# Start addresses of matmul operands in a fused attention and feed-forward kernel

## The reference

```python
x = x + tanh(g_xattn[0]) * L0_xattn(layernorm(x), ctx, ctx, W, b)
x = x + tanh(g_ffn[0])   * L0_ffn(layernorm(x), Wg, Wu, Wd)       # 8 experts, 256 -> 1024 -> 256
x = x + tanh(g_xattn[1]) * L1_xattn(layernorm(x), ctx, mask, ...)  # 8 heads of 64
x = x + tanh(g_ffn[1])   * L1_ffn(layernorm(x), wg, W, b)          # routed, 8 experts

def L0_ffn(x, Wg, Wu, Wd):       # the part with the split products
    acc = 0
    for wg, wu, wd in zip(Wg, Wu, Wd):
        acc += (silu(x @ wg) * (x @ wu)) @ wd
```

## The kernel before

| operand | arena | start |
|---|---|---|
| `xop_hi`, `xop_lo` (moving, gate and up) | `sb` | 1376 behind a multiple of 2048 |
| `w_hi`, `w_lo`, `wd_hi`, `wd_lo` (weights of gate, up, down), one block of 128 | `sb` | 352 behind a multiple of 512 |
| `hid_hi`, `hid_lo` (moving, down) | `st` | 256 behind a multiple of 2048 |
| `t_hi`, `t_lo` of T1, T2, T4 (moving, down), T3 lies in `hid` | `sx` | 128 behind a multiple of 2048 |
| `wds_hi`, `wds_lo` (weights, summed, down), one block of 128 | `sx` | 128 behind a multiple of 512 |

## Time and profile before

### The profile page before, as it was taken

The page is one execution under the profiler, slowest core; times in us unless marked ns, Lnnn a source line. Parts: engine busy times, 40 slices in busy tenths (PEclk is TensorE's granted clock), DMA queues, the critical chain, the costliest instruction groups (busy, mean ns, idle before and its releaser), DMA issues.

```text
span 1258.8 us, 18431 instructions
## 1 busy us (share of the span) xinstructions
PE 1232.6 (98%) x6152; PEld 995.4 (79%) x6152; DVE 1054.3 (84%) x1775; ACT 729.2 (58%) x1509; POOL 880.5 (70%) x833
## 2 busy tenths in 40 slices
PE   7999999999999999999999999999999999999998
PEld 5778888888888888888888888888888887787775
DVE  5887889898899999999999999888999974667546
ACT  2455566656666666666666666666566545545543
POOL 3735688888887888888877888888888626443435
PEclk9999999999999999999999999999999999999999
DMA  4020200000110000000000000000100330000131
GB/s 137 26 92 1 94 26 26 26 26 26 41 36 26 26 26 26 26 26 26 26 26 26 26 26 26 26 26 31 42 29 1 117 118 1 18 26 10 35 98 63
DMA packets 42366, 48.28 MB, mean 38 GB/s; under 512 B 4239, under 2 KB 40143, under 8 KB 42015
## 3 DMA queue, kind: packets, MB, share of 16 engines
q1 hardware_dynamic: 38720, 43.07, 10.4%
q0 software_dynamic: 1440, 3.41, 0.8%
q10 hardware_dynamic: 2111, 0.63, 0.2%
HBM read 37.36 MB, written 10.29 MB: 38 GB/s over the span
## 4 chain that ended last, share of the span: by engine, by line
PE 91%; DVE 4%; ACT 3%; issue 1%; DMA 0%; POOLq 0%; ACTq 0%; POOL 0%; DVEq 0%
PE bank L1307 25%; PE bank L1308 25%; PE bank L1309 25%; ACT PC L1050 2%; PE bank L1545 2%; PE bank L1554 1%; PE bank L1269 1%; PE bank L1707 1%; PE bank L1724 1%; PE bank L1251 1%; DVE nmC L2101 1%; PE bank L1529 1%; PE bank L1213 1%; PE bank L1657 1%; PE bank L1479 1%
## 5 line engine op out<-in xcount | busy, mean ns | idle before, releaser
L1307 PE MATMUL bank<-xop_hi,w_hi 128*128 128x512 f32 x896 | 351.9, 393 | 1.7 <-ACT half_g L948 1.2
L1308 PE MATMUL bank<-xop_lo,w_hi 128*128 128x512 f32 x896 | 352.4, 393 | 0.0
L1309 PE MATMUL bank<-xop_hi,w_lo 128*128 128x512 f32 x896 | 351.4, 392 | 0.0
L1958 DVE TENSOR_TENSOR hid_lo<-hid,hid_hi 128x512 fp32r<-128x512 f32 x228 | 220.2, 979 | 14.1 <-ACT hid_hi L972 9.8
L1307 PEld LDWEIGHTS bank<-xop_hi,w_hi 128*128 128x128 f32 x896 | 168.9, 188 | 42.4 <-ACT half_g L948 1.5
L1308 PEld LDWEIGHTS bank<-xop_lo,w_hi 128*128 128x128 f32 x896 | 168.6, 188 | 38.2
L1309 PEld LDWEIGHTS bank<-xop_hi,w_lo 128*128 128x128 f32 x896 | 168.6, 188 | 37.7
L972 ACT CAST hid_hi<-hid 128x512 fp32r<-128x512 f32 x228 | 140.8, 622 | 57.9 <-DVE hid L1950 57.9
L956 ACT ACTIVATE s<-bank 128x512 f32<-128x512 f32 x128 | 78.3, 612 | 102.5 <-PE bank L1309 102.5
L1307 PE MATMUL bank<-hid_hi,wd_hi 128*128 128x512 f32 x344 | 136.2, 396 | 0.6 <-DVE hid_lo L1958 0.6
L1308 PE MATMUL bank<-hid_lo,wd_hi 128*128 128x512 f32 x344 | 136.2, 396 | 0.0
(11 more groups left out here) (273 smaller groups left out, 2615.1 us busy)
## 6 DMA issues: line engine op xcount, KB each, us to landing
raw_gu<-in_L_ffn_Wg_dram SPq DMA_DIRECT2D x32, 256.0 KB, 2.7
raw_gu<-in_L_ffn_Wu_dram SPq DMA_DIRECT2D x32, 256.0 KB, 3.1
raw_d<-in_L_ffn_Wd_dram SPq DMA_DIRECT2D x32, 256.0 KB, 3.7
slots<-empty_row SPq DMA_DIRECT2D x1, 2080.0 KB, 11.1
xr<-slots SPq DMA_DIRECT2D x8, 260.0 KB, 4.5
x_res<-in_x_dram SPq DMA_DIRECT2D x4, 512.0 KB, 5.3
x_mid<-x_res SPq DMA_DIRECT2D x1, 2048.0 KB, 9.2
x_res<-x_mid SPq DMA_DIRECT2D x4, 512.0 KB, 5.4
```

The lines of the kernel that those rows point to most:

```text
L1307: mm(ps, w, a, start=start, stop=False, skip_group_check=True)
L1308: mm(ps, w, a_low, start=False, stop=False, skip_group_check=True)
L1309: return mm(ps, w_low, a, start=False, stop=True, skip_group_check=True)
L1958: nc.vector.tensor_tensor(out=hid_lo[n % 2][h][:], in0=hid[h][:], in1=hid_hi[n % 2][h][:].bitcast(F32), op=ALU.subtract).then_inc(lo_ready ...
```

## The change

No instruction is added, taken out or moved, on any engine: in both programs 11441 instructions stand in the same order with the same shapes, waits and signals. Tiles lie at other addresses. Constants name a row of 2048 bytes and two remainders; `Arena.align` moves an arena's next address up to a remainder.

```diff
+ROW_BYTES = 2048
+OPERANDS_AT = 0
+STATIONARY_AT = 256
...
+    def align(self, residue):
+
+        self.at += (residue - self.at) % ROW_BYTES
+        assert self.at <= self.end, (self.at, self.end)
...
-        x_res = keep.take("x_res", [P, NT, D], F32)
...
+        desc = keep.take("desc", [P, CT, E], F32)
+        keep.align(OPERANDS_AT)
+        x_at = keep.at
+        x_res = keep.take("x_res", [P, NT, D], F32)
         a0_at = keep.at
...
+        sums_at = sa.at + (OPERANDS_AT - sa.at) % ROW_BYTES
...
-        st = Arena(nc, keep.at, sa.at)
+        st = Arena(nc, keep.at, sums_at)
...
         hid_hi, hid_lo = [], []
+        st.align(OPERANDS_AT)
...
-        sx = Arena(nc, base, base + 4 * NT * D)
+        sx = Arena(nc, x_at, x_at + 4 * NT * D)
...
-        m_acc = {i: sm.take(f"m_acc{i}", [P, CH], F32) for i in ("M1", "M5", "M6")}
-
-        sb = Arena(nc, sa.at, end)
+        m_acc = {i: sm.take(f"m_acc{i}", [P, CH], F32) for i in ("M1", "M5", "M6", "M7")}
+
+        sb = Arena(nc, sums_at, end)
         acc = sb.take("acc", [P, KB, T], F32)
+        assert sb.at % ROW_BYTES == OPERANDS_AT
...
         for i in range(2):
+            if i == 0:
+                sb.align(STATIONARY_AT)
             w_at.append(sb.at)
```

More of the change, by code:

```diff
@@ L175, in flamingo_kernel @@
         keep = Arena(nc, base, end)
-        x_res = keep.take("x_res", [P, NT, D], F32)
+        LANES = NC + 3
+        LN_FRONT, LN_FRONT2, LN_ROUTE = range(NC, LANES)
         ident = keep.take("ident", [P, P], F32)
@@ L184, in flamingo_kernel, with norm_lanes @@
         V0 = keep.take("V0", [KH, 2 * B, D], F32)
+        stats, mv, ve, rstd = [], [], [], []
+        def norm_lanes(of):
+            for i in of:
+                stats.append(keep.take(f"stats{i}", [P, CT, 6], F32))
+                mv.append(keep.take(f"mv{i}", [P, CT, 2], F32))
+                ve.append(keep.take(f"ve{i}", [P, CT], F32))
+                rstd.append(keep.take(f"rstd{i}", [P, CT], F32))
+        norm_lanes(range(NC))
         v0_end = keep.at
@@ L191, in flamingo_kernel @@
         betac = keep.take("betac", [P, KB], F32)
[L193 to L198, removed]
+        norm_lanes(range(NC, LANES))
         wgr = keep.take("wgr", [P, KB, E], F32)
@@ L204, in flamingo_kernel @@
         tg_ffn = keep.take("tg_ffn", [P, 2], F32)
-        desc = keep.take("desc", [P, CT, E], F32)
         slot0 = keep.take("slot0", [P, CT, E], F32)
@@ L277, in flamingo_kernel @@
         hid.update({h: sb.take(f"hid{h}", [P, CH], F32) for h in BLOCKS[2:]})
-        m_acc["M7"] = sb.take("m_accM7", [P, CH], F32)
         pre = Arena(nc, raw_at, raw_end)
```

## The result

| | before | after |
|---|---|---|
| timed runs, us | 1256.47, 1257.12, 1257.2, 1258.66 | 1239.03, 1239.21, 1239.24, 1245.24 |
| median, us | 1257.16 | 1239.22 |
| ratio after / before, 95% interval | | 0.9866 [0.9842, 0.9889] |
| profiled execution: span (its own timed run) | 1258.8 (1258.66) | 1237.3 (1239.03) |

What follows compares the result with a forecast made beforehand. PE's matmul spacing was taken as the bound; 16.9 us from split matmuls plus 0.6 from queries, 17.5 together, took the span from 1258.8 to 1241.3 and the median to 1240 us, range 1204 to 1265.

Steps and rivals of the forecast that it cites:

- PE's spacing is the bound: Split-product stage: PE bounds, matmuls starting 230.7 ns apart; DVE second at 91%, rising to 93% without becoming the bound.
- The extra goes with the distance of moving operand and next weights: Split products: extra matmul time follows the operand's address less that of the weights loaded beside it, not waits.
- always a multiple of 64 (and of 256): Distances after the change, 256 or 0, would settle at 389 ns because long matmuls were 32 off a multiple of 64.
- The size: Split matmuls: 4120 x 4.1 ns = 16.9 us saved, 4.1 taken between 3.8 by record lengths and 4.4 by starts.
- the quiet 389: Record length in ns of xop_lo where xop products follow xop products; all split matmuls were to fall to it.
- queries: Query matmuls, at a constant distance of 96: 96 x (233.1 - 226.7) ns = 0.6 us saved.
- As if it took a few matmuls to settle: Split products: a matmul of distance 0 shortly behind one at a bad distance is still long.
- Wholly apart (379 ns, 1210 us): Rival, chance 0.23: at distance 256 load and operand never meet, split matmuls fall to 379 ns; 1202 to 1220 us.
- Slower by distance, count over 512: Rival, chance 0.19: 256 is the far end of 512 bytes, split matmuls never settle, 233.1 ns; 1267 us, up to 1290.
- Addresses not the cause: Rival, chance 0.12: long split matmuls come from down's banks or tiles DVE and POOL read; nothing moves, 1257 us.
- no visible tie to their addresses: Moved `m_accM7` and small tiles: DVE and POOL lengths would not change, cost nothing; DVE additions a tenth longer would erase the gain.

Runs made afterwards that it cites:

- e5: The kernel after with the weights on a multiple of 512 (`STATIONARY_AT = 0` in place of 256), every distance 0; 1239.50 us.
- e2: The kernel after with the weights at 64 in place of 256 behind a multiple of 512, distance 448 (0 before wds loads); 1265.10 us.
- e4: The kernel after with operands and weights both 32 bytes later, distances still 256 and 0; 1240.12 us.
- e12: The kernel before with only hid_hi and hid_lo moved, 96 bytes later; 1245.31 us, ratio 0.9911.
- e8: The kernel before with the weight tiles 256 bytes later, so distances keep their remainder of 256; 1257.58 us.
- e3: The kernel after with the weights at 32 in place of 256 behind a multiple of 512, distance 480 (0 before wds loads); 1267.77 us.
- e10: The kernel after with the second and third matmul of each product loading 64 weight columns, not 128, and writing 64 rows; 1250.43 us.
- e11: The kernel after with 64-column loads in two of three matmuls and the weights at 64 in place of 256 (distance 448); 1260.24 us.
- e1: The kernel before with the arena `sb` 32 bytes later, making every distance a multiple of 128; 1257.37 us, ratio 1.0004.

## Why the prediction was right, and where it was not

*PE's spacing is the bound.* Right. The 4.1 ns per matmul are gone and the span followed; PE waits for other engines about as long as before (six waits, 3.43 us against 3.33), though DVE's share in the steady part went to 93% as worked out.

*The extra goes with the distance of moving operand and next weights.* Right, and now shown: the same instructions in the same order have 226.7 ns or 233.2 by it alone (e5, e2), the operand's own start has no part in it (e4), and the weights are those loaded beside the matmul (e12).

*"always a multiple of 64 (and of 256)".* This step failed in its first half, without harm to the forecast. The sentence "of the distances seen the one that is a multiple of 64 over a long stretch settles there" took the modulus from rows in which every bad distance was 32 off such a multiple. 448, 128 and 384 are multiples of 64 as well and stay at 233.3, 232.2 and 233.4 ns; 320 at 228.9. The modulus is 256 (e8, e5), and the change's 256 and 0 are both 0 in it. That the change's distances fit the true modulus too was luck as far as the argument goes. Had the change set the weights off by 64, the same argument would have given 1240 us, and the chip gave 1265 (e2).

*The size.* 4120 x 4.1 = 16.9 us was measured as 4065 x 4.10 = 16.7 in the gaps counted here; queries 0.6 as 0.5. That all kinds fall to the quiet 389 ns was right. The choice of 4.1 came out to the digit, which is partly luck: the measure by lengths was too small (the six groups now have a mean of 389.4 ns, 3.4 less than before's without the half clock), the one by starts too large (the quiet spacing is 226.7, not the 226.3 read from rounded starts), and the middle evened it out.

*"As if it took a few matmuls to settle".* Right, and it carries half of the gain: of before's 16.7 us over the quiet spacing, 8.6 lie in the 1440 counted gaps off a multiple of 256, and 8.1 in the 2625 at 0 that stand behind them.

*Wholly apart (379 ns, 1210 us).* This did not come: a distance of 256 has 226.67 ns and one of 0 has 226.69. No run shows 379 ns for a matmul of 512 columns, and the 10 ns of this sum were the author's estimate, the quiet 389 less the 379 of the earlier trace rows; in the kernel after the xop_lo, hid_lo and wds records from 200 to 900 us have 388 to 390 ns. The records of 256 fp32 columns are still at 379 ns; what the 10 ns between them and 389 are stays open, as no distance tried gives them back.

*Slower by distance, count over 512.* Such a price exists, but not at 256. The size was right: 233.1 ns was named for a distance that never settles, and e2 and e3 have 233.0 to 233.2. They came to 1265 and 1268 us (2.5 us of the latter from its half-clock start) where the rival had 1267.

*Addresses not the cause.* Refuted: 226.7 against 233.2 ns at equal clock, a difference of 3%, by addresses alone. For matmuls of this kind where the next weights lie changes the pace. That less to load did not make e10 faster (229.4 ns against 226.7) speaks against a plain price per byte loaded, but does not settle it, as e10 changes the matmuls as well.

*DVE and POOL, "no visible tie to their addresses".* The runs agree for the tiles that change place. DVE's additions into `m_accM` have a median of 676 ns before and after, its `stats` operations on x_res 409 and 410 and those on `mv` 149 and 149. Of the eight additions on POOL that read `m_accM`, seven differ by 6 ns or less, and the seventh in time went from 1288 to 1802 ns; e2 has these tiles where the kernel after has them, and there it takes 1298 ns. DVE's hid_lo became longer (979 to 1052 ns), but e2 has hid where the kernel after has it and 955 ns, and in e4 hid begins 32 bytes later and has 1052 ns as in the kernel after.

*Of the profiled executions.* The sum was made against a span of 1258.8 us, of which 2.5 us were its half-clock start. The nine matmuls there were left out of the gain. No run shows the change's distance of 256 at half clock; what the runs show is the same spacing of 426 or 427 ns at three other distances, 0 (nine gaps in before), 480 (eight in e3) and 448 (nine in e11), so among these three the distance had no price. The two spans differ by 21.5 us, which overstates the change by these 2.5 us and by the scatter behind the stage.

## What to carry to other kernels

When matmul records of one shape come in several lengths at full clock, the same each time at the same place, look at the moving operand's start less the start of the weights loaded beside it. Here the remainder of this distance by 256 had to be 0, whatever the starts themselves (e4, e5). One line that moved the hid tiles was worth 11 us where the whole change was worth 18 (e12), because a bad distance slows seven or more matmuls behind it too (231.9 to 228.0 ns on average for the first and the seventh there, against 226.7). Addresses of one layout that vary together fit several moduli, so choose a distance that is good under every one of them.

## What the runs showed of the hardware

- fp32r matmuls of 128 x 512 with a 128 x 128 load each (188 ns) start 226.7 ns apart at best, at full granted clock: 389 ns records. With a distance at any other remainder of 256 that was tried (32, 64, 128, 160, 192, 224) it is 228.9 to 234.4 ns, a loss of up to 3%.
- The slow state lasts: after the last bad distance the next seven matmuls are slow as well in e12, not evenly (228 to 234 ns), and up to nine or ten in the kernel before and e1. A burst behind a wait starts slow and settles (the queries after the change: 232.5, then 226.7 ns).
- The weights that count are those loaded beside the matmul, for the one behind it: 235 ns in all 56 places of e12 where those alone are at a bad distance behind a quiet stretch.
- With half as wide loads and matmuls in two of three, the loads are done sooner (134 ns) and yet the matmuls of a settled stream are slower (229.4 against 226.7), those of an unsettled one faster (231.2 against 233.2); why was not found.
- At half clock the starts are 0.43 us apart. Such a start cost the profiled execution before 2.5 us, about the 0.2% to either side in the ratio's 95% interval, and those of e3 and e11 had it as well (first 70 gaps 22.5 and 22.4 us against 19.9 to 20.0 in the kernel after and the other experiments). So read the clock of the first products in both traces before two spans are compared.
